# Two attention layers, experts and a binary FFN on one core: the waits that pace GpSimd's scatters, and the wait for their landing

## The chip, the core and the metric

The kernel runs on one core of a Trainium2 chip as one program. The metric is the device time of an execution in microseconds (us); "before" is the median of three runs. A profile of one execution gives the rows below.

## The reference

Four parts follow one another, each added to x (4 batches of 1024 tokens, 256 wide, f32), each on a layer norm of x: a cross attention with 77 keys and a mask, a mixture of experts with a shared expert, a second cross attention, and a feed-forward part with binary weights.

```python
x = x + _L0_xattn_ref(_layernorm(x), ctx, ctx, mask, ...)   # 16 heads of 16, 77 keys
x = x + _L0_ffn_ref(_layernorm(x), Wg, W1, W2, W3, Ws1, Ws2, Ws3)
x = x + _L1_xattn_ref(_layernorm(x), ctx, ctx, ...)
x = x + _L1_ffn_ref(_layernorm(x), k0, k1, k2, s0, s1, s2)
# in _L0_ffn_ref:
scores = softmax(xf @ Wg); weights, indices = top_k(scores, 4)      # 32 experts
for e in range(E):          # the tokens that chose e, at most C = 4 * T * 4 / 32
    out = swiglu(xf[tok], W1[e], W2[e], W3[e]) * w[:, None]
    y = y.at[tok].add(out)
z = swiglu(xf, Ws1, Ws2, Ws3)                                       # the shared expert
return y + z
```

## The kernel before

The 4096 tokens are 32 tiles of 128 rows, and four tiles make a macro tile (eight of them, m = 0 to 7). x stays in SBUF. The program is a row of blocks, and at each block's end all engines meet in a barrier: `front` (norm and queries of the first attention), `attend` (first attention), `route` (shared expert and routing), `experts`, `combine`, `attend` again (second attention) and `ffn`. Behind `attend` and `experts` the function `retire` also clears semaphores and meets in a second barrier; between `route` and `experts` it isn't called.

**Attention.** `attend` is written as 35 steps (`body`), software-pipelined over the tiles. In step t TensorE (PE) makes the scores of tile t+1, turns the probabilities of tile t in three pieces (L1008), and does `values` of tile t-1 (L1019): 30 matmuls of 51 f16 columns, each with its own 128x128 weights, 20 from PHT and 10 from PLT, into psO. Its last matmul raises `pv_done`. VectorE (DVE) opens step t with `norm` of tile t-2 (L867, L871), which waits for `pv_done` of step t-1 and raises `normed`; then come two `maximum` (L855, each raises `max_ready`), and three `low` (L862, each raises `lo_out`), with the residual between them. PE's `shift` (L997) waits for `max_ready`, so the next probabilities start from norm.

**Routing beside it.** In the first attention `Gate` does the router of macro tile m while later tiles are attended: norm by GpSimd (`power`, L1147 to L1152), turn and logits on PE (L1198, L1208), `pick` and `index` on DVE, `ranks` on PE (L1216, 14 matmuls of 32 columns), `place` and `slots` on DVE (L1270 to L1284). This ends in 16 slot numbers for each of 128 partitions. Then GpSimd (POOL) copies the macro tile's normed rows to the experts' regions of `x_rows` in HBM by 16 indirect DMAs (`scatter`, L1160): each takes 128 rows of 1072 bytes, one to a partition. Macro tiles 0 to 3 are scattered in the attention from step 4m + 15 on, four scatters to a step. `in_step` there says what each waits for: the first `normed` (norm of this step done), the others the three `lo_out` of the step. Of macro tile 4, `CUT` scatters are issued in the attention's last steps; what is left of it and macro tiles 5 to 7 are scattered in `route`. There another `in_step` paces them by PE's progress, in groups of seven to each shared-expert macro tile. The scatters of all eight macro tiles are 128.

**Route.** PE computes the shared expert of macro tile b (L1551 up, L1568 down), with the logits and ranks of macro tiles 6 and 7 in its first two turns. Its 30-odd groups are f32 matmuls of 256 or 512 columns. SyncE (SP) loads weights and the second attention's keys and values, stores zero rows behind each expert's last row ("tails", L1396) and loads W2 (L2041). At its end SP waits for the tails and POOL for the landing of every scatter.

**Experts.** SP fetches 128 rows of `x_rows` for each of 160 expert tiles (`fetch`, L1642), eight ahead. PE turns the first (L1750) and goes on from there; every expert tile's result is scattered to `y_rows` by POOL (L1657).

**The second attention** is the same `attend` without gate and scatters.

Two pieces of text that the diff doesn't show:

```python
def norm(t, u):                       # DVE, at the head of step t + 2
    dve.wait_ge(pv_done, t + 1)
    ...
def values(t, u):                     # PE, in step t + 1
    pe.wait_ge(normed, t); pe.wait_ge(lo_out, NG * t + NG)
```

Of the kernel before, what the change touches and what calls it, by code (L numbers as in the profile page):

```python
# [24 lines left out]
KC = D // P  # L25
TOKENS = BATCH * SEQ
TILES = TOKENS // P
# [26 lines left out]
GATED_EARLY, SCATTERED_EARLY, TURNED_EARLY = 6, 4, 7  # L54
CUT = 6
TURN_AT, LOGITS_AT, PICK_AT, RANKS_AT, SCATTER_AT = 8, 9, 11, 13, 15
STEPS = 7
KEYS_AT = 1
# [60 lines left out]
def build(nc, a, out):  # L119
# [605 lines left out]
    def attend(w, masked, clear_outputs, load_ahead, tail=None, gate=None):  # L725
# [73 lines left out]
        with nc.Block() as block:  # L799
# [20 lines left out]
            def _(pool):  # L820
# [12 lines left out]
                if gate:  # L833
# [3 lines left out]
                    def in_step(t, j):  # L837
                        if j == 0:
                            pool.wait_ge(normed, min(t - 1, TILES))
                        else:  # L840
                            pool.wait_ge(lo_out, min(NG * t + j, NG * TILES))
                    for m in range(SCATTERED_EARLY):
# [241 lines left out]
    class Gate:  # L1084
# [3 lines left out]
        def __init__(self, st):  # L1088
            def keep(n):
# [27 lines left out]
                keep(n) for n in ("chosen", "c_done", "ranks_read", "slots_ready", "own", "edges", "based"))  # L1117
            self.wg_in, self.w1_in = (keep(n) for n in ("wg_in", "w1_in"))
            self.scattered = [keep(f"scattered_{i}") for i in range(ROWBUFS)]
            self.own = None  # L1120
# [6 lines left out]
        def load(self, sp):  # L1127
            sp.dma_start(self.wg, a["wg"].rearrange("(c p) n -> p c n", p=P)).then_inc(self.wg_in, 16)
            sp.dma_start(self.w1, a["ws1"].rearrange("(c p) n -> p c n", p=P)).then_inc(self.w1_in, 16)

        def recycled(self, eng, m):
# [206 lines left out]
    def route(gate, counts, plan_all, own_f, next_w, load_down):  # L1338
# [25 lines left out]
            sem(s) for s in ("h_done", "silu", "hs", "z_done", "z_added", "w2_in", "plan_ready", "plan_spread", "plan_read", "w3_in"))  # L1364
        tails_s, tails_st = sem("tails_ready"), sem("tails_stored")
        own_s, plan_own = sem("own"), sem("plan_own")
# [7 lines left out]
        with nc.Block() as block:  # L1374

            @block.sync
            def _(sp):
# [19 lines left out]
                for m in range(PLAN_AT, MACROS):  # L1397
                    down(m)
                sp.wait_ge(tails_st, 16 * EXPERTS)

            @block.gpsimd
            def _(pool):
                kv.blanks(pool)

                def in_step(n):
                    b, j = divmod(n, STEPS)
                    if j in (0, 1, 4, 5):
                        pool.wait_ge(h_done, min(4 * b + (1, 2, 0, 0, 3, 4)[j], 4 * MACROS))
                    elif j in (2, 3) and b:
                        pool.wait_ge(z_done, 2 * b + j - 3)  # L1410
                gate.power(pool, MACROS - 1)
                for m in range(SCATTERED_EARLY, MACROS):
                    first = CUT if m == SCATTERED_EARLY else 0
                    gate.scatter(pool, m, first, MT * TOPK, lambda i: in_step((m - SCATTERED_EARLY) * MT * TOPK + i - CUT))
                for b in range(ROWBUFS):
                    pool.wait_ge(gate.scattered[b], SCATTERS * len(range(b, MACROS, ROWBUFS)))

# [186 lines left out]

    def experts(W13, W2, w_loaded, plan_all, own_f, binary):
        st = ExitStack()
# [22 lines left out]
        with nc.Block() as block:  # L1629

            @block.sync
            def _(sp):
                regs = [sp.alloc_register(f"first_row_{n}") for n in range(AHEAD)]

                def fetch(j, u, g):
# [6 lines left out]
                    sp.dma_start(XG[:, u, :], x_rows[ds(row, P), :]).then_inc(gathered[u], 16)  # L1642

                for j in range(ETILES):
                    fetch(j, j % AHEAD, j // AHEAD)
                    if j == AHEAD:
                        binary.load_first(sp)
                    if j == SECOND_LOAD:
                        binary.load_second(sp)
# [372 lines left out]
    with whole:  # L2022
# [24 lines left out]
        gating.close()  # L2047
        experts(W13, W2, (w_loaded, 16 * (2 * KC + 2 * MACROS)), plan_all, own_f, BinaryWeights())
        moe.close()
# [44 lines left out]
```

## Time and profile before

| what | value |
|---|---|
| median of 3 runs | 1307.51 us (1304.01 to 1314.53) |
| the profiled execution | 1310.99 us, span 1309.2 us |
| PE / DVE / ACT / POOL busy | 1179.9 / 742.6 / 516.9 / 414.3 us |
| scatters L1160 | 128, 967 to 972 ns each at the least and the median |
| first attention, route, experts (first work to last, by the rows) | 47 to 310, 311 to 417, 425 to 720 us |
| second attention | 800 to 965 us |

The busy time of an engine is a sum over stages, and it tells little of a stage in which the engines hand work to one another. How long a step of the attention lasts is read as the distance between two starts of L867. In the rows a bracket behind a row is the time for which the engine was idle before it, and what ended that; "remote" is a semaphore whose sender the profile doesn't name. An x2 behind a row counts instructions that follow each other closely, and the duration is then that of all of them.

### The profile page before, as it was taken

The page shows a single profiled execution, that of the slowest core. Times are in us where ns is not written, and L with a number is a line of the kernel's source. Part 1 is how long each engine was busy: PE and PEld are TensorE (multiplying, and loading weights), DVE is VectorE, ACT ScalarE, POOL GpSimd, SP SyncE. Part 2 cuts the span into 40 slices and gives each one's busy share as a digit, 9 for nine tenths or more (in the row PEclk, how much of TensorE's full clock was granted, in tenths as well). Part 3 has the DMA queues.
Part 4 walks back from the last instruction along what each step waited for, and adds up shares of the span by engine and source line. Part 5 has one row for each costly group of instructions (what it writes and reads, how often), then busy time and mean ns, then how long its engine had stood idle before and what let it go on. Part 6 is the DMA issues. An engine that isn't in the chain of part 4 may idle for free. (4 is left out here: it accounts for less than half of the span.)

```text
span 1309.2 us, 26064 instructions
## 1 busy us (share of the span) xinstructions
PE 1179.9 (90%) x8528; PEld 809.7 (62%) x8528; DVE 742.6 (57%) x1969; ACT 516.9 (39%) x1110; POOL 414.3 (32%) x513
## 2 busy tenths in 40 slices
PE   7799988887996899999998078999989999999998
PEld 4378766565553787777777045888855555554554
DVE  4277877764633466656566594888863343424331
ACT  6555644443211344433433155666532122213221
POOL 5260255554465355555456264300000000000000
PEclk9889999986998899999999588999999999999999
DMA  9199211112296555454442750000000000000000
GB/s 183 18 296 394 111 64 69 64 64 82 73 220 215 157 159 154 134 179 131 133 139 70 309 212 14 2 3 2 2 1 1 17 17 17 1 16 16 17 17 17
DMA packets 100993, 123.93 MB, mean 95 GB/s; under 512 B 34224, under 2 KB 76291, under 8 KB 100871
## 3 DMA queue, kind: packets, MB, share of 16 engines
q1 hardware_dynamic: 87047, 87.98, 23.0%
q0 software_dynamic: 13824, 34.38, 7.4%
q8 instruction: 71, 1.16, 0.4%
q14 instruction: 51, 0.42, 0.1%
HBM read 61.78 MB, written 64.72 MB: 97 GB/s over the span
## 5 line engine op out<-in xcount | busy, mean ns | idle before, releaser
L1971 PE MATMUL psA<-H,B 128*128 128x512 f16 x1024 | 223.5, 379 | 0.0
L1898 DVE SCALAR_TENSOR_TENSOR H<-psA,H 128x512 f16<-128x512 f32 x128 | 88.3, 690 | 208.3 <-ACT H L1939 208.3
L1657 POOL DMA_INDIRECT y_rows<-YB,pair x160 | 155.5, 972 | 147.5 <-DVE YB L1712 78.4
L1939 ACT ACTIVATE H<-psA 128x512 f16<-128x512 f32 x128 | 76.4, 597 | 252.7 <-PE psA L1971 252.7
L1971 PEld LDWEIGHTS psA<-H,B 128*128 128x128 f16 x1024 | 100.1, 98 | 119.4
L1767 PE MATMUL psH<-W,XT 128*128 x640 | 168.7, 387 | 1.6 <-issue 1.5
L940 ACT ACTIVATE PHT<-psT 128x512 f16<-128x512 f32 (+1 forms) x192 | 94.4, 524 | 129.9 <-PE psT L1008 129.9
L862 DVE TENSOR_TENSOR PLT<-psT,PHT 128x512 f16<-128x512 f32 (+1 forms) x192 | 113.9, 595 | 30.2 <-ACT PHT L940 27.3
L208 POOL TENSOR_SCALAR var<-mv 128x4 f32<-128x4 f32 x24 | 11.2, 467 | 371.2 <-DVE mv L202 370.2
L1160 POOL DMA_INDIRECT x_rows<-B,slot_s x96 | 96.2, 1002 | 84.9 <-PE psH L1551 23.1
L1767 PEld LDWEIGHTS psH<-W,XT 128*128 128x128 f32 x640 | 111.2, 194 | 12.1 <-issue 3.2
L1008 PE MATMUL psT<-ident,PR 128*128 128x128 f32 x640 | 102.9, 289 | 11.4 <-issue 5.2
L855 DVE TENSOR_REDUCE mx<-psS 128x8 fp32r<-128x616 f32 x128 | 95.9, 790 | 28.4 <-PE psS L988 28.1
L1669 ACT ACTIVATE XT<-psX 128x256 f32<-128x256 f32 x160 | 61.3, 383 | 122.7 <-PE psX L1750 90.5
L1781 PE MATMUL psY<-QT,HT 128*128 x320 | 99.8, 394 | 0.0
L1723 DVE COPY HT<-psT 128x128 f32<-128x128 f32 x159 | 46.3, 291 | 92.5 <-PE psT L1775 55.8
L932 ACT ACTIVATE PR<-psS 128x616 f32<-128x616 f32 x128 | 83.2, 690 | 38.9 <-PE psS L997 38.6
L1008 PEld LDWEIGHTS psT<-ident,PR 128*128 128x128 f32 x640 | 71.2, 145 | 34.6 <-issue 26.3
L1712 DVE TENSOR_SCALAR YB<-psY,to_gate 128x256 f32<-128x256 f32 x160 | 77.0, 482 | 11.5 <-PE psY L1781 10.5
L1750 PE MATMUL psX<-ident,XG 128*128 128x128 f32 x320 | 62.5, 278 | 15.9 <-DMA XG<-x_rows 13.2
L223 PE MATMUL psX<-ident,XN 128*128 128x128 f32 x184 | 28.4, 305 | 50.5 <-ACT XN L457 50.5
L997 PE MATMUL psS<-mx,minus_ident 128*128 128x312 f32 x256 | 62.9, 355 | 10.1 <-DVE mx L855 9.9
(248 smaller groups left out, 2054.2 us busy)
## 6 DMA issues: line engine op xcount, KB each, us to landing
XG<-x_rows SPq DMA_DIRECT2D x160, 134.0 KB
y_rows<-zero_row SPq DMA_DIRECT2D x4, 4096.0 KB, 27.2
G<-y_rows SPq DMA_DIRECT2D x7, 2048.0 KB, 10.2
x_rows<-zero_row SPq DMA_DIRECT2D x33, 134.0 KB, 7.4
X<-in_x SPq DMA_DIRECT2D x8, 512.0 KB
QT<-in_w SPq DMA_DIRECT2D x16, 256.0 KB
out_x<-OUT SPq DMA_DIRECT2D x8, 512.0 KB
y_rows<-YB,pair POOLq DMA_INDIRECT x160
```

The lines of the kernel that those rows point to most:

```text
L855: dve.tensor_reduce(m, half(h), X_AXIS, ALU.max).then_inc(max_ready, 1)
L862: dve.tensor_tensor(PLT[u][:, lo:hi], piece(t, g), PHT[u][:, lo:hi], ALU.subtract).then_inc(lo_out, 1)
L932: act.activation(PR[u][:, h * HH:(h + 1) * HH, 0:KEYS].rearrange("p (r j) k -> p r j k", r=2), half(h), ACT.Exp, scale=SCALE).then_inc(exp ...
L940: act.activation(PHT[u][:, lo:hi], piece(t, g), ACT.Copy).then_inc(hi_out, 1)
L1008: last = pe.transpose(piece(t, g)[:, c - lo], flat[:, c * P:(c + 1) * P], ident[:])
L1160: pool.indirect_dma_start(x_rows[:, :], bass.IndirectOffsetOnAxis(ap=self.slot_s[m % ROWBUFS][:, i:i + 1], axis=0), self.rows[m % ROWBUFS] ...
L1657: pool.indirect_dma_start(y_rows[:, :], bass.IndirectOffsetOnAxis(ap=pair[u // HALF][:, u % HALF:u % HALF + 1], axis=0), YB[u][:], None, b ...
L1712: dve.tensor_scalar(YB[u][:], psY[u % 2][:], to_gate[u // HALF][:, u % HALF, 1:2], None, ALU.mult).then_inc(y_out, 1)
L1767: last = pe.matmul(psH[v][:], XT[v][:, c], w13[c][:, ds(e * (2 * HID), 2 * HID)], start=c == 0, stop=c == KC - 1)
L1781: pe.matmul(psY[v][:], HT[v][:], w2[:, ds(e * D, D)], start=True, stop=True).then_inc(y_done, 1)
L1898: dve.scalar_tensor_tensor(out=H[layer][1][:, o], in0=psA[k % 4][:], scalar=0.0, in1=H[layer][0][:, o], op0=ALU.max, op1=ALU.subtract).the ...
L1971: last = pe.matmul(psA[k % 4][:], W[:, c, o * P:(o + 1) * P], src[part][:, c], start=n == 0, stop=n == 2 * n_in - 1)
```

## The change

In the first attention, the four scatters of a step wait for four other things: the first as before for `normed`; the second for the step's second `maximum`; the third for the step's second `low`; the fourth for `pv_done` of the step's `values`. Ten scatters of macro tile 4 are issued in the attention and not six, so six and not ten are left for `route`. In `route` no scatter waits for PE's progress any longer; each batch of 16 still waits for its rows, its weights and its slots. The waits for the landing of all scatters and all tails move from the end of `route` (POOL and SP) to SP's queue in `experts`, ahead of the first fetch.

```diff
--- before.py
+++ after.py
@@ -52,9 +52,8 @@
 ROWBUFS = 4
 SCATTERS = 16 * MT * TOPK
 GATED_EARLY, SCATTERED_EARLY, TURNED_EARLY = 6, 4, 7
-CUT = 6
+CUT = 10
 TURN_AT, LOGITS_AT, PICK_AT, RANKS_AT, SCATTER_AT = 8, 9, 11, 13, 15
-STEPS = 7
 KEYS_AT = 1
@@ -837,8 +836,12 @@
                     def in_step(t, j):
                         if j == 0:
                             pool.wait_ge(normed, min(t - 1, TILES))
+                        elif j == 1:
+                            pool.wait_ge(max_ready, min(2 * t + 4, 2 * TILES))
+                        elif j == 2:
+                            pool.wait_ge(lo_out, min(NG * t + 2, NG * TILES))
                         else:
-                            pool.wait_ge(lo_out, min(NG * t + j, NG * TILES))
+                            pool.wait_ge(pv_done, min(t, TILES))
                     for m in range(SCATTERED_EARLY):
                         gate.scatter(pool, m, 0, MT * TOPK, lambda i: in_step(m * MT + SCATTER_AT + i // MT, i % MT))
                         gate.power(pool, m + MT - 1)
@@ -1116,6 +1119,7 @@
+            self.tails_st = keep("tails_stored")
@@ -1127,6 +1131,11 @@
+        def all_rows(self, sp):
+            sp.wait_ge(self.tails_st, 16 * EXPERTS)
+            for b in range(ROWBUFS):
+                sp.wait_ge(self.scattered[b], SCATTERS * len(range(b, MACROS, ROWBUFS)))
@@ -1396,24 +1405,15 @@
                 for m in range(PLAN_AT, MACROS):
                     down(m)
-                sp.wait_ge(tails_st, 16 * EXPERTS)
 
             @block.gpsimd
             def _(pool):
                 kv.blanks(pool)
 
-                def in_step(n):
-                    b, j = divmod(n, STEPS)
-                    if j in (0, 1, 4, 5):
-                        pool.wait_ge(h_done, min(4 * b + (1, 2, 0, 0, 3, 4)[j], 4 * MACROS))
-                    elif j in (2, 3) and b:
-                        pool.wait_ge(z_done, 2 * b + j - 3)
                 gate.power(pool, MACROS - 1)
                 for m in range(SCATTERED_EARLY, MACROS):
                     first = CUT if m == SCATTERED_EARLY else 0
-                    gate.scatter(pool, m, first, MT * TOPK, lambda i: in_step((m - SCATTERED_EARLY) * MT * TOPK + i - CUT))
-                for b in range(ROWBUFS):
-                    pool.wait_ge(gate.scattered[b], SCATTERS * len(range(b, MACROS, ROWBUFS)))
+                    gate.scatter(pool, m, first, MT * TOPK, lambda i: None)
@@ -1641,6 +1641,7 @@
                         sp.wait_ge(met, 2 * g + u // HALF - 1)
                     sp.dma_start(XG[:, u, :], x_rows[ds(row, P), :]).then_inc(gathered[u], 16)
 
+                gate.all_rows(sp)
                 for j in range(ETILES):
                     fetch(j, j % AHEAD, j // AHEAD)
                     if j == AHEAD:
```

(`experts` takes `gate` as a further argument, and `tails_st` in `route` is now `gate.tails_st`.)

Three places on the engines' instruction lists show it. First POOL's list in the first attention, at the first macro tile's scatters (`x_rows<-B_23`). Before:

```order
L1160 DMA x_rows<-B_23,slot_s 69760x268 [waits gate_slots_ready,normed_172,gate_top_out,gate_xn_ready]
L1160 DMA x_rows<-B_23,slot_s 69760x268 [waits lo_out_169] x3
L1160 DMA x_rows<-B_23,slot_s 69760x268 [waits normed_172]
L1160 DMA x_rows<-B_23,slot_s 69760x268 [waits lo_out_169] x3
L1160 DMA x_rows<-B_23,slot_s 69760x268 [waits normed_172]
```

Now:

```order
L1169 DMA x_rows<-B_23,slot_s 69760x268 [waits gate_slots_ready,normed_172,gate_top_out,gate_xn_ready]
L1169 DMA x_rows<-B_23,slot_s 69760x268 [waits max_ready_164]
L1169 DMA x_rows<-B_23,slot_s 69760x268 [waits lo_out_169]
L1169 DMA x_rows<-B_23,slot_s 69760x268 [waits pv_done_170]
L1169 DMA x_rows<-B_23,slot_s 69760x268 [waits normed_172]
```

Of the three scatters that waited for `lo_out`, one is left, one went ahead of it and one behind the step's `values`. Second, POOL's list from the attention's end into `route`, now (before, four scatters fewer stood ahead of the first of these branches):

```order
L1169 DMA x_rows<-B_23,slot_s 69760x268 [waits pv_done_170]
L1169 DMA x_rows<-B_23,slot_s 69760x268 [waits normed_172]
L1169 DMA x_rows<-B_23,slot_s 69760x268 [waits max_ready_164]
L798 UNCONDITIONAL_BRANCH
L132 ISA [waits barrier_Pool_Activation_PE_DVE_SP_gather]
...
L1169 DMA x_rows<-B_23,slot_s 69760x268 [waits gate_slots_ready,gate_top_out,gate_xn_ready]
L1169 DMA x_rows<-B_23,slot_s 69760x268 x5
L1169 DMA x_rows<-B_23,slot_s 69760x268 [waits gate_slots_ready,gate_top_out,gate_xn_ready]
L1169 DMA x_rows<-B_23,slot_s 69760x268 x15
...
L1383 UNCONDITIONAL_BRANCH
```

The last scatters of the attention now stand behind `pv_done` and `normed` of its last tile, and the branch that ends `route` has no waits; before it read:

```order
L1374 UNCONDITIONAL_BRANCH [waits gate_scattered_2,gate_scattered_3,gate_scattered_1,gate_scattered_0]
```

Third, SP's list where `experts` begins, now:

```order
L1383 UNCONDITIONAL_BRANCH
L1631 UNCONDITIONAL_BRANCH [waits barrier_Pool_Activation_PE_DVE_SP_release]
L1637 TENSOR_LOAD plan_all [waits gate_scattered_2,gate_scattered_1,gate_scattered_3,gate_scattered_0,gate_tails_stored]
L1638 ISA
L1642 DMA XG<-x_rows 128x268
```

The load of the row numbers, and so every fetch, carries the waits that stood ahead of the barrier.

## Rows read from the trace of the kernel before

**Rows 1.** Timeline of VectorE, first attention: start us, duration us, instruction [idle before]; heads of steps.

```profile
129.70 0.22 DVE L867 RECIPROCAL rden<-psO 128x16 f32<-128x16 f32 x1
...
156.71 0.25 DVE L867 RECIPROCAL rden<-psO 128x16 f32<-128x16 f32 x1
...
239.57 0.26 DVE L867 RECIPROCAL rden<-psO 128x16 f32<-128x16 f32 x1 [2.27 <-remote]
...
247.53 0.26 DVE L867 RECIPROCAL rden<-psO 128x16 f32<-128x16 f32 x1 [3.45 <-remote]
...
291.15 0.25 DVE L867 RECIPROCAL rden<-psO 128x16 f32<-128x16 f32 x1
```

**Rows 2.** Waits, 150 to 300 us: us in total, times, longest.

```profile
DVE rden L867 <- remote: 32.9, 15, 3.5
```

**Rows 3.** Timeline of the second attention: end of `values` and the next step's head.

```profile
867.32 0.18 PE L1019 MATMUL psO<-V,PLT 128*128 128x51 f16 x1
...
867.68 0.25 DVE L867 RECIPROCAL rden<-psO 128x16 f32<-128x16 f32 x1
```

**Rows 4.** Timeline of PE and POOL in two steps of the first attention with scatters.

```profile
237.09 0.19 PE L1019 MATMUL psO<-V,PLT 128*128 128x51 f16 x1
...
237.86 0.97 POOL L1160 DMA_INDIRECT x_rows<-B,slot_s  x1 [0.30 <-issue]
...
241.09 0.97 POOL L1160 DMA_INDIRECT x_rows<-B,slot_s  x1 [2.25 <-DVE CX L871]
...
243.02 0.21 PE L1019 MATMUL psO<-V,PHT 128*128 128x51 f16 x2
...
243.09 0.97 POOL L1160 DMA_INDIRECT x_rows<-B,slot_s  x1 [1.04 <-DVE PLT L862]
...
245.65 0.97 POOL L1160 DMA_INDIRECT x_rows<-B,slot_s  x1 [0.30 <-issue]
```

**Rows 5.** Timeline of DVE: the end of `slots` in a step without scatters.

```profile
156.63 0.17 DVE L1284 CAST slot_s<-B 128x16 int32<-128x16 f32 x1
```

**Rows 6.** Timeline where the first attention ends and `route` begins: POOL, DVE, SP.

```profile
300.81 0.97 POOL L1160 DMA_INDIRECT x_rows<-B,slot_s  x1 [0.31 <-issue]
...
302.79 0.26 DVE L867 RECIPROCAL rden<-psO 128x16 f32<-128x16 f32 x1 [3.82 <-remote]
...
309.65 0.17 DVE L1284 CAST slot_s<-B 128x16 int32<-128x16 f32 x1
...
311.45 0.38 SPq L1378 DMA_DIRECT2D B<-in_ws  x1
```

**Rows 7.** Timeline where `experts` ends and `combine` begins: POOL, SP.

```profile
719.07 0.97 POOL L1657 DMA_INDIRECT y_rows<-YB,pair  x1 [0.30 <-issue]
...
725.78 0.90 SPq L673 DMA_DIRECT2D G<-y_rows  x2
```

**Rows 8.** Timeline of `route`: DVE and PE, early and in the middle.

```profile
326.59 0.29 DVE L1270 TENSOR_TENSOR B<-psR,base 128x128 f32<-128x128 f32 x1 [2.23 <-remote]
...
327.49 5.38 PE L1551 MATMUL psH<-QT,B 128*128 128x512 f32 x8
...
332.70 3.62 PE L1568 MATMUL psZ<-w,HS 128*128 128x256 f32 x16
...
370.49 3.62 PE L1568 MATMUL psZ<-w,HS 128*128 128x256 f32 x16
```

**Rows 9.** Timeline where `route` ends and `experts` begins: SP, DVE, POOL, PE.

```profile
400.22 9.81 SPq L2041 DMA_DIRECT2D QT<-in_w  x12
...
413.77 0.69 DVE L1471 TENSOR_TENSOR X<-X,psZ 128x512 f32<-128x512 f32 x1 [0.78 <-PE psZ L1568]
...
416.10 0.97 POOL L1160 DMA_INDIRECT x_rows<-rows,slot_s  x1 [0.30 <-issue]
...
424.58 0.94 SPq L1642 DMA_DIRECT2D XG<-x_rows  x2
...
426.72 0.69 PE L1750 MATMUL psX<-ident,XG 128*128 128x128 f32 x2 [12.99 <-DMA XG<-x_rows]
```

More of the change, by code:

```diff
@@ L1364, in route @@
             sem(s) for s in ("h_done", "silu", "hs", "z_done", "z_added", "w2_in", "plan_ready", "plan_spread", "plan_read", "w3_in"))
-        tails_s, tails_st = sem("tails_ready"), sem("tails_stored")
+        tails_s, tails_st = sem("tails_ready"), gate.tails_st
         own_s, plan_own = sem("own"), sem("plan_own")
@@ L1603, in route, with experts @@
         st.close()
-    def experts(W13, W2, w_loaded, plan_all, own_f, binary):
+    def experts(W13, W2, w_loaded, plan_all, own_f, binary, gate):
         st = ExitStack()
@@ L2047, in build @@
         gating.close()
-        experts(W13, W2, (w_loaded, 16 * (2 * KC + 2 * MACROS)), plan_all, own_f, BinaryWeights())
+        experts(W13, W2, (w_loaded, 16 * (2 * KC + 2 * MACROS)), plan_all, own_f, BinaryWeights(), gate)
         moe.close()
```

## The prediction

> **What bounds the kernel now.** I read the page's slices first, then the waits, then the timeline of the places that the edits touch. About 1% (13 us) is what a measurement of this kernel can tell from no change. The sums are made against the profiled execution, 1310.99 us, which lies 3.5 above the median 1307.51.
>
> The first attention hands work round between the engines, and a step is read from one L867 to the next. Four steps without scatters take 156.71 - 129.70 = 27.0 us. From there to 291.15 lie 16 steps, in which four macro tiles are scattered: 134.4 us, 33.6 for four [rows 1]. The router's work is the same in both. In the waits DVE stands at L867 for a "remote" semaphore 15 times, 32.9 us in all [rows 2]. L867 waits for `pv_done`, the end of PE's `values`. In the second attention, with no scatters, `values` ends at 867.32 + 0.18 = 867.50 and L867 starts 0.18 later [rows 3]. In the first one `values` is recorded as ended at 237.28, and L867 starts at 239.57 [rows 4, 1]: 2.29 us. That stretch is the time in which POOL runs the last of its back-to-back scatters, start 237.86, and L867 follows 1.71 after that start. So my reading is that a group of small matmuls with many weight loads doesn't finish, or its count isn't seen, while scatters follow one another without a gap; the recorded end of PE is modelled and hides this. DVE waits, and everything of the next step hangs on its norm.
>
> Where do the three scatters behind `lo_out` fall? In the step of 239.57 the first goes at 241.09 behind the norm, the second at 243.09 behind the first `low`, the fourth at 245.65; a scatter lasts 0.97 and the next one starts 0.30 behind it, so 1.28 each [rows 4]. `values` begins at 243.02. Three back-to-back scatters lie on it, all ahead of `pv_done`, and the next L867 comes at 247.53, 1.88 behind the last one's start [rows 1, 4]. The step is 7.96 long.
>
> In `route` the f32 groups don't show this: L1568 x16 takes 3.62 us at 332.70 among spaced scatters and 3.62 at 370.49 among back-to-back ones [rows 8]. A small group does: DVE waits 2.23 "remote" for ranks (L1270, 326.59), and the L1551 group behind it is recorded at 5.38 us for eight matmuls [rows 8].
>
> The end of `route`: DVE's last work ends at 413.77 + 0.69 = 414.46, POOL's last scatter at 417.07. The first fetch is issued at 424.58 and PE starts at 426.72 after 12.99 us idle [rows 9].
>
> **Attention, spacing.** One of three scatters that lay ahead of `pv_done` now lies behind it. Take `pv_done` at 0: the fourth scatter starts at about 0.8 (the start of 241.09 is 1.52 behind L867 at 239.57 and L871 lies between, so a wake-up takes 0.8), the first of the next step at 2.1 by POOL's spacing, then 3.4 and 4.6, since their waits (second maximum, second `low`) are met by then. `values` lies at 3.5 to 4.4. The release comes 1.75 (mean of 1.71 and 1.88) behind the last: 6.4. Before, it was 7.96, and the difference is one spacing, 1.28, and some. Per four steps I get 6.4 for two steps with nothing else, and 15 for the two that also carry the router's work, of which one is bound by DVE anyway: in the cycle without scatters, `slots` ends at 156.63 + 0.17 and L867 is there at 156.71 [rows 5, 1]. Together some 28 to 28.5 against 33.6: 5.1 to 5.6, times four is 20 to 22. I take **-20**. The most it can give is 134.4 - 108.0 = 26.4 (four cycles at 27.0); the least, if the wait comes of any scatter near `values` and not of their row, is 0, or worse by nothing that these rows show, since each step has the same four scatters.
>
> **Attention, the end.** Four more scatters run behind `normed` and `pv_done` of the last tile. The last one of before starts at 300.81; DVE ends at 309.65 + 0.17 = 309.82, and `route`'s first work is at 311.45, 1.6 later: POOL wasn't the bound [rows 6]. Now the row of POOL begins with the last `pv_done`, seen at 302.79 [rows 6]: four scatters from 0.5 on end at about 307.1. A block whose end hangs on a scatter is seen twice: experts' last scatter ends at 720.04 and `combine` starts at 725.78, 5.7 later [rows 7]; route's 417.07 and 424.58, 7.5 later, there with waits for the landing [rows 9]. 307.1 + 5.7 = 312.8 to 307.1 + 7.5 = 314.6, against 311.45: +1.4 to +3.2. I take **+2**; 0 if POOL's drain runs beside DVE's tail, 4 at worst.
>
> **Route, unpaced scatters.** 54 scatters at 1.28 are 69 us: from 314 to 383, not to 417.07. The f32 groups cost nothing by [rows 8]. The ranks of macro tile 7, which sat between spaced scatters, now fall into a row of them: one wait like that of macro tile 6, 2.23 us, with 1.8 of PE behind it (5.38 for x8 of 512 columns against 3.62 for x16 of 256, the same columns). I take **+2**, bounds 0 and 5. The transfers to HBM are fewer beside W2 at the end than before, which costs nothing I can see.
>
> **Route, the end.** POOL and SP no longer hold the barrier. What is last is DVE's 414.46. At the attention's end it took 1.6 from DVE's last work to the next block's first [rows 6], there with a clearing that isn't done here: 414.46 + 0.5 to 1.6 is 415.0 to 416.1, against 424.58: -8.5 to -9.6. The moved waits are long met: the last scatter ends at about 383 and the tails are ahead of the W2 loads in SP's queue [rows 9]. SP has the load of W2 behind it at 400.22 + 9.81 = 410.03. Queued behind the moved waits are the row numbers and every fetch; if these waits weren't met, PE would wait for them as now. I take **-9**.
>
> Sum: -20 + 2 + 2 - 9 = -25: **1286 profiled, 1283 as a median**.
>
> **A rule against it.** The rows show DVE held 2.3 us behind `values` only where scatters run [rows 1, 3, 4]. The Trainium skill (SBUF — State Buffer, "SBUF: two separate sides") says that inside the engines' side only the port pair of DVE and GpSimd contends, and that TensorE never waits on anyone. By it PE couldn't be held by a scatter, and moving scatters past `pv_done` would give nothing in the attention. The sum doesn't use it; it is the first rival's mechanism.
>
> **Rivals.**
> 1. Spacing gives nothing. L867's "remote" wait comes with the four scatters of a step, not with three in a row: what holds it is their number, and the new fourth scatter, behind `pv_done`, only joins the next step's three, so POOL runs the same row of four. For it: POOL is busy 5.1 us of a step either way, and after the change no gap is left in the row. Against: 6.4 of POOL's row ends earlier. Time: +2 + 2 - 9 = -5: **1302.5**.
> 2. `values` isn't held at all any more, for its row of scatters is broken: four cycles at 27.0, -26.4 + 2 + 0 - 9 = -33: **1274**. Against: POOL has the work of 5.1 us in 6.7, so a scatter lies on `values` always.
> 3. Slower. In `route`, unpaced scatters hold PE's groups as they do in the attention, which stretched four steps by 33.6/27.0 = 1.24: 69 us would hold 69 - 69/1.24 = 13.4 more. With no gain in the attention: -9 + 2 + 13.4 = +6.4; with the ranks at +5 as well, +11: **1314 to 1319**. It decides from 5 us of PE held on. For it: the 2.23 and the 5.38 [rows 8]. Against: 3.62 in both kinds of stretch.
> 4. The change doesn't spread the scatters: the second and third waits are met when POOL comes to them, so the four go out in one row from `pv_done` on. My step already counts with that; where the row then also reaches past the next `pv_done`, POOL paces the steps and it ends as rival 1.
>
> **Chances.** Forecast 0.50 (1276 to 1292: the attention -26 to -12, its end 0 to +4, the ranks 0 to +5). Rival 2 0.17, rival 1 and 4 0.25 (1295 to 1306), rival 3 0.08. The range: 1271 (all of rival 2 but its last few us) to 1302, which leaves out rival 3, a third of rival 1 and little else: under 2 in 10. Faster by over 1% (under 1294.4): the forecast, rival 2 and a little of 1: 0.70. Within 1%: 0.23. Slower by over 1% (over 1320.6): only the upper end of rival 3 and what no row shows: 0.07.
>
> **What would show it.** L867 to L867: 27.5 to 29 us for four steps between 156 and 285, and the "remote" total of L867 well under 20 us; 33 says rival 1, 27 rival 2. The last L1160 of `route` at about 375 to 385, L1568 x16 still at 3.62; a longer one is rival 3. The gap between DVE's last work of `route` and the first L1642 at 0.5 to 1.6 us. The gap between the attention and `route`, from DVE's last work to L1378, at 1.6 to 5. I am wrong if small groups are held by something other than rows of scatters, if the landing of W2 or of the scatters comes late, or if the fetches' first rows meet a queue that the earlier scatters filled.

## The result, and the profile after

The change is slower: 1329.36 us (median of 4 runs, 1326.96 to 1341.93) against 1309.59, ratio 1.0172 with a 95% interval of 1.0094 to 1.0249. The forecast was 1283. The experiments then showed that these runs belong to one of two conditions, and that what scatters cost TensorE differs between them by some 50 us for the very same kernel; I call them **held** (the runs of before at 1304 to 1315 us) and **free** (at 1255 to 1263 us). In the free one the change is not told apart from before: 1255.72 against 1257.74, ratio 0.9988, 0.9946 to 1.0029. First the profile of the change in the held condition (the profiled execution 1330.2 us, span 1328.5; lines moved by 3 to 9).

VectorE's timeline, heads of steps, as in [rows 1]. A cycle below is four steps, in which the 16 scatters of one macro tile are issued.

```profile
156.64 0.25 DVE L870 RECIPROCAL rden<-psO 128x16 f32<-128x16 f32 x1
...
162.98 0.26 DVE L870 RECIPROCAL rden<-psO 128x16 f32<-128x16 f32 x1
...
169.69 0.26 DVE L870 RECIPROCAL rden<-psO 128x16 f32<-128x16 f32 x1 [0.85 <-PE psO L1022]
...
176.72 0.26 DVE L870 RECIPROCAL rden<-psO 128x16 f32<-128x16 f32 x1 [0.75 <-PE psO L1225]
...
189.33 0.25 DVE L870 RECIPROCAL rden<-psO 128x16 f32<-128x16 f32 x1
...
286.27 0.25 DVE L870 RECIPROCAL rden<-psO 128x16 f32<-128x16 f32 x1
```

Three steps of this cycle last 6.3, 6.7 and 7.0 us (forecast: 6.4 for two of them), where they lasted about 7.9. The fourth, with the logits and ranks, lasts 12.6 against 9.6; in the four cycles it takes 12.6, 10.9, 12.6 and 10.9 us. Four cycles take 286.27 - 156.64 = 129.6 us, and took 134.4 [rows 1].

The attention's end and the beginning of `route`, as in [rows 6]: VectorE, SyncE.

```profile
306.23 0.17 DVE L1293 CAST slot_s<-B 128x16 int32<-128x16 f32 x1
```

```profile
311.04 0.38 SPq L1387 DMA_DIRECT2D B<-in_ws  x1
```

4.6 us from the one's end to the other, against 1.6.

Waits, 310 to 440 us (us in total, times, longest):

```profile
DVE B L1248 <- remote: 30.9, 1, 30.9
...
DVE B L1279 <- remote: 7.9, 1, 7.9
```

L1248 reads the logits of macro tile 7. The timeline of PE around them, and of POOL:

```profile
325.44 1.94 PE L1217 MATMUL psX<-B,QT 128*128 128x32 f32 x16 [0.93 <-ACT QT L1518]
327.22 5.38 PE L1551 MATMUL psH<-QT,B 128*128 128x512 f32 x8
...
342.55 0.58 PE L1568 MATMUL psZ<-w,HS 128*128 128x256 f32 x1 [1.51 <-issue]
344.65 0.59 PE L1568 MATMUL psZ<-w,HS 128*128 128x256 f32 x1 [1.51 <-issue]
347.45 0.59 PE L1568 MATMUL psZ<-w,HS 128*128 128x256 f32 x1 [2.21 <-issue]
349.56 1.01 PE L1551 MATMUL psH<-QT,B 128*128 128x512 f32 x1 [1.53 <-issue]
352.35 1.01 PE L1551 MATMUL psH<-QT,B 128*128 128x512 f32 x1 [1.78 <-issue]
```

```profile
360.57 0.97 POOL L1169 DMA_INDIRECT x_rows<-B,slot_s  x1 [0.30 <-issue]
361.85 0.97 POOL L1169 DMA_INDIRECT x_rows<-B,slot_s  x1 [0.30 <-issue]
376.77 0.97 POOL L1169 DMA_INDIRECT x_rows<-rows,slot_s  x1 [13.95 <-DVE slot_s L1293]
```

```profile
365.67 0.29 DVE L1248 TENSOR_REDUCE B<-psX 128x4 f32<-128x128 f32 x1 [30.86 <-remote]
```

The logits group is recorded as ended at 327.38 and VectorE reads it at 365.67, 2.9 us after the row of scatters pauses (361.85 + 0.97). The trace also keeps the times at which semaphores were raised: the count that L1248 waits for stands at 365.64. So it isn't VectorE that is late; the count itself comes 38.3 us behind the recorded end. Meanwhile TensorE gets through one matmul in 2.1 to 2.8 us, waiting for "issue". The windows of 334 to 362 and 362 to 370 us (PE, PEld, DVE, ACT, POOL busy; granted clock; DMA; GB/s) show what that does:

```profile
334.00:362.00 28.00, 8.24 (x14) 3.00 (x12) 0.77 (x2) 0.00 (x0) 21.30 (x23) 0.58 0.29 105
362.00:370.00 8.00, 1.41 (x2) 0.84 (x3) 3.72 (x21) 3.65 (x10) 0.82 (x1) 0.50 0.09 34
```

PE works 8 of 28 us, and the granted clock falls from 2.4 to 1.2 GHz in that stretch. POOL stopped only because the last slots hung on those logits.

The end of `route`, as in [rows 9]: VectorE, SyncE, PE.

```profile
448.77 0.69 DVE L1471 TENSOR_TENSOR X<-X,psZ 128x512 f32<-128x512 f32 x1 [0.78 <-PE psZ L1568]
450.60 2.35 SPq L1642 DMA_DIRECT2D XG<-x_rows  x4
...
452.77 0.48 PE L1751 MATMUL psX<-ident,XG 128*128 128x128 f32 x1 [4.04 <-DMA XG<-x_rows]
```

From VectorE's end to the first fetch it is now 1.1 us; it was 10.1. This part came as forecast.

| change in us, before to after | held | free |
|---|---|---|
| up to the head of step 156 | -0.1 | -1.4 |
| from there to VectorE's end in the attention | -3.3 | 0.0 |
| to `route`'s first load | +3.0 | +4.7 |
| to VectorE's end in `route` | +35.4 | -0.8 |
| to the first fetch | -9.0 | -9.0 |
| experts, to the first load of `combine` | -8.0 | +1.3 |
| the rest | +1.3 | +0.2 |
| span | +19.3 | -5.1 |

(The free column is from one profiled execution each, 1259.65 and 1254.55 us.) Why the experts are 8 us shorter in the held column isn't settled: in the five other held profiles, that of before among them, they last 298 to 307 us, in free ones 280, so they are held too, and by a varying amount; what sets that amount was not tested.

### The profile page after: what moved, and what is told of

The parts are those of the page before. It is cut to its first block and busy times, and to the rows that moved or that the text cites. A ratio compares the mean times of both kernels' runs of the same rounds, so it can differ in the third digit from the quotient of the medians.

```text
span 1328.5 us, 26058 instructions
## 1 busy us (share of the span) xinstructions
PE 1176.0 (89%) x8528; PEld 815.3 (61%) x8528; DVE 742.9 (56%) x1969; ACT 517.1 (39%) x1110; POOL 411.1 (31%) x513
## 5 line engine op out<-in xcount | busy, mean ns | idle before, releaser
L858 DVE TENSOR_REDUCE mx<-psS 128x8 fp32r<-128x616 f32 x128 | 96.0, 792 | 29.7 <-PE psS L991 29.6
L935 ACT ACTIVATE PR<-psS 128x616 f32<-128x616 f32 x128 | 82.5, 689 | 36.7 <-PE psS L1000 36.0
L1551 PE MATMUL psH<-QT,B 128*128 128x512 f32 x128 | 64.9, 653 | 18.6 <-ACT SG L1514 12.4
L1042 PE MATMUL psM<-wo,CT 128*128 128x256 f32 x256 | 69.9, 397 | 0.6 <-ACT CT L949 0.5
```

The costliest lines, as they stand in the source:

```text
L858: dve.tensor_reduce(m, half(h), X_AXIS, ALU.max).then_inc(max_ready, 1)
L935: act.activation(PR[u][:, h * HH:(h + 1) * HH, 0:KEYS].rearrange("p (r j) k -> p r j k", r=2), half(h), ACT.Exp, scale=SCALE).then_inc(exp ...
```

## The experiments

Each is an edit of the kernel before unless it says otherwise. Ratios are against before in the same comparison.

**1. The parts alone.** `land`: only the landing waits are moved. `route`: only

```diff
-  gate.scatter(pool, m, first, MT * TOPK, lambda i: in_step((m - SCATTERED_EARLY) * MT * TOPK + i - CUT))
+  gate.scatter(pool, m, first, MT * TOPK, lambda i: None)
```

`attn`: only the four waits in the attention and `CUT = 10`. `attn_land`: `attn` and `land`.

> Only the waits for the landing of scatters and tails are moved to SyncE's queue behind the barrier; scatters are issued and paced as before. Theory: this part works as predicted and is worth the gap at route's end. POOL's last scatter still ends at about 417, so the barrier is left by POOL 1 to 5 us behind that: first fetch at 418 to 422 instead of 424.6, 3 to 6 us less in all. Rival: the drain of POOL and not the wait for the landing makes the gap; then the first fetch stays at 424 and the time is the same within 1 us.

> Only the pacing in route is taken away (48 + 10 scatters back to back); attention and landing waits as before. Theory: an unbroken row of scatters starves TensorE, and this one edit is the loss: the logits of macro tile 7 are seen over 25 us late, route's matmuls come one by one at about 2 us, and the kernel is 20 to 30 us slower than before. Rival: it takes the ten scatters of the attention with it (other positions, four more at the end); then this kernel is within 8 us of before.

> Only the attention's part: the new waits of the second to fourth scatter and ten instead of six scatters of macro tile 4; route paced and landing waits as before. Theory: the three steps without router work get 1.1 us shorter each, the fourth 1 to 3 us longer, so the attention ends about 3 us earlier and the kernel is 2 to 5 us faster than before. Rival: four scatters fewer in route also let route end 6 us earlier, since POOL is the last there: 8 to 10 us faster.

> Attention's part and moved landing waits together, route paced: the change without the unpaced scatters. Theory: the parts add up: route ends with DVE at 411 to 414, the first fetch comes 1 to 2 us behind it, 10 to 14 us faster than before, and 30 us faster than the change. Rival: the paced scatters still end last in route; then only 5 to 8 us faster than before.

Before took 1258.49 us here (22 runs). `land` 1258.2, ratio 0.9998 (0.9987 to 1.0009): nothing, as its rival said. POOL's last scatter still ends at 385.6 and the first fetch comes at 391.5. `route` 1251.45, 0.9929 (0.9907 to 0.9950): some 7 to 9 us faster, where 20 to 30 us slower was expected. `attn` 1258.22, 0.9982 (0.9965 to 0.9998) and `attn_land` 1256.21, 0.9980 (0.9962 to 0.9998): some 2 us, and under 5 by the intervals. All four have cycles of 26.8 us and no remote wait at L867. So neither the hold nor its cure could be seen here, and my account of the first profile stood untested.

**2. The change and the kernel before again.**

> The change itself, once more. In the four partial kernels no wait of VectorE behind TensorE's small groups was seen while scatters ran, and the route part alone was 7 us faster than before; in the change's first profile such waits were 5 to 31 us long. Theory: whether rows of scatters hold TensorE's completions depends on the chip or its condition at the time, not on the combination of the parts. Then either this run has no such wait and is 6 to 10 us faster than before, or it has them and is 15 to 25 us slower, and the kernel before beside it shows the same condition (four-step cycle 27 or 33.5 us). Rival: only the combination of parts does it; then the change is slower here while the kernel before has cycles of 27 us.

> The kernel before, once more, for its profile beside that of the change on the same chip. Theory: it has remote waits at L867 (cycle 33.5 us, about 1308 us) exactly where the change is slower, and none (cycle 27 us, about 1258 us) where it is faster. Rival: its cycle says nothing about the change's result.

The two numbers are given above: free, cycles of 26.8 in both. VectorE's timeline in the kernel before, of a profile without any hold:

```profile
156.70 0.25 DVE L867 RECIPROCAL rden<-psO 128x16 f32<-128x16 f32 x1
...
163.04 0.26 DVE L867 RECIPROCAL rden<-psO 128x16 f32<-128x16 f32 x1
...
168.73 0.26 DVE L867 RECIPROCAL rden<-psO 128x16 f32<-128x16 f32 x1
...
174.40 0.24 DVE L867 RECIPROCAL rden<-psO 128x16 f32<-128x16 f32 x1
...
183.55 0.25 DVE L867 RECIPROCAL rden<-psO 128x16 f32<-128x16 f32 x1
...
263.90 0.25 DVE L867 RECIPROCAL rden<-psO 128x16 f32<-128x16 f32 x1
```

263.90 - 156.70 = 107.2 us for the 16 steps that took 134.4 in [rows 1], with the same scatters, four to a step. The combination isn't needed for the hold, nor enough for it. The span differs by 1309.2 - 1257.9 = 51.3 us: 29.7 from the head at 156.7 to VectorE's end in the attention, 0.2 from there to the first fetch, 21.7 in the experts, and -0.3 elsewhere. The two stages in which POOL scatters beside many short groups of TensorE hold it all; the second attention and `ffn` are alike. The scatters' packets take as long in both: in the queue's rows of the 16 steps (packets, MB, share of 16 engines), before in its first profile over 133.3 us, and again over 105.3 us,

```profile
q0 software_dynamic: 2991, 8.58, 17.9%
```

```profile
q0 software_dynamic: 2928, 8.37, 22.1%
```

133.3 x 16 x 0.179 / 2991 = 0.128 us a packet, and 105.3 x 16 x 0.221 / 2928 = 0.127. So it isn't slower transfers that hold TensorE.

The kept traces differ in one more way. Both of before record all 26064 instructions, but not as many raised semaphores: from the head at 156.7 to the attention's end 1067 held and 1678 free, in `route` 1250 and 2238, in the experts 3007 and 6851, and elsewhere the same within one (1314 and 1314 ahead of it, 2186 and 2187 behind). Most of the missing ones are the DMAs' own. On the page it shows as a fetch without a time to its landing, first before, then before again:

```profile
XG<-x_rows SPq DMA_DIRECT2D x160, 134.0 KB
```

```profile
XG<-x_rows SPq DMA_DIRECT2D x160, 134.0 KB, 2.5
```

All six held profiles of this document lack this time, and all fourteen free ones have it (2.3 to 2.6 us). Records are missing exactly in the stages with indirect DMAs, so either raised semaphores as such are disturbed there, or their recording is. Whether an execution without a recording knows the hold at all is a rival that no run here tests.

**3. A later start of the row.** `late`: `route`'s edit, and POOL waits ahead of it for the read of the last logits (`pool.wait_ge(gate.l_shift, MACROS)`). `late_b` is the same once more.

> Route's scatters back to back as in the change, but the row starts only when VectorE has read the last logits (13 us later); attention and landing waits as before. Two conditions have been seen: one in which scatters hold TensorE's completions (before about 1308 us), one in which they don't (before about 1258 us). In the first: if only small groups of matmuls open the backlog, the logits wait of 31 us is gone, one wait of the last ranks remains, and route is within 5 us of before, the kernel 2 to 8 us faster; if f32 groups are held as well, route is 15 us or more longer. In the second: the row ends at about 373 instead of 359, still ahead of VectorE's last work, so as fast as the unpaced kernel, 5 to 8 us faster than before.

> Route's scatters back to back, but the row starts only when VectorE has read the last logits, once more; the rest as before. Where scatters hold TensorE (before at about 1313 us): if only groups of many small matmuls open the backlog, the logits wait of 31 us is gone and what is left is the ranks of the last macro tile, a wait of 2 to 25 us by VectorE at L1270, and L1568 x16 stays at 3.6 us outside it: route 105 to 125 us long. If f32 groups are held as well by an unbroken row, they come one matmul at a time over the whole row of 74 us and route is 135 us or longer, as without the late start (145). Where they don't hold it: 103.7 as before seen.

Free both times. `late` 1252.06, 0.9941 (0.9921 to 0.9962), `late_b` 1255.25 beside 1259.77 (one run). The row ended at 375 to 376 (expected: 373), ahead of VectorE's 385. What it does in the held condition stays untried.

**4. The change without its attention part** (`route_land`), and **pauses between scatters.** Ahead of each scatter of route (`gap`), or of the second to fourth of an attention step in place of its wait (`attn_gap`), two memsets of a spare 128x32 tile:

```diff
+        def pause(self, pool):
+            for _ in range(2):
+                pool.wait_ge(self.gap_s, self.gaps)
+                pool.memset(self.gap[:], 0.0).then_inc(self.gap_s, 1)
+                self.gaps += 1
```

> Route's scatters back to back and the landing waits moved, attention and the six scatters of macro tile 4 as before: the change without its attention part. Where scatters don't hold TensorE: the moved waits give nothing more, since POOL and the landing are 25 us ahead of VectorE already; 6 to 8 us faster than before, as the route part alone, and 3 to 5 us faster than the change, which pays for four scatters behind the attention's last tile. Rival: the two edits add up, and it is 9 us or more faster. Where scatters do hold TensorE: 20 us or more slower than before.

> Route's scatters unpaced, but two small memsets of POOL that wait for one another ahead of each, so that no two scatters stand back to back; the rest as before. Where scatters hold TensorE (before at about 1308 us): if it is the unbroken row that does it, the logits wait is gone and route ends with POOL at about 410 to 415; if POOL's scatters hold it at any spacing, it is over 15 us slower. Where they don't (before about 1258 us): 58 scatters at 1.9 us end at about 395, behind VectorE's last work, and the kernel is within 3 us of before.

> In the attention the second to fourth scatter of a step wait for nothing but two small memsets of POOL ahead of each; the rest as before. Where scatters hold TensorE: if an unbroken row does it, the remote waits at L867 go and the four-step cycle falls from 33.5 us to 28 to 30, the kernel 14 to 20 us faster; otherwise it stays at 33. Where they don't: the cycle is 26.8 us as without any scatters, and the time that of before within 2 us.

Free. `route_land` 1252.09, 0.9945 (0.9925 to 0.9965): the parts of the end don't add up, since the early end of the scatters alone removes the gap. `gap` 1273.1 beside 1258.72, and `attn_gap` 1277.38: both expectations of "no more than 2 or 3 us" were wrong. The gap between scatters grew from 0.30 to 0.95 us, 1.92 a scatter. In `route` 58 of them end at 398.7 and the fetch at 406.5 waits for them; in the attention 7.0 us a step is more than the 6.7 that a step lasts, and the last two cycles came to 31.4 and 32.4. Where nothing is held, pauses only make POOL the bound.

**5. One burst, and rows of eight.** `burst`: in the attention, of a macro tile's 16 scatters only the first waits. `row8`: `route` unpaced, with six such memsets ahead of every eighth scatter.

> In the attention only the first scatter of each macro tile waits for its step; the other 15 follow back to back, 20 us in a row, and POOL rests for the remaining steps of the cycle. The rest as before. Where scatters hold TensorE (before at about 1308 us): if an unbroken row is what does it, three steps of a cycle stand together behind one wait of L867 of 10 us or more, and the cycle is over 33 us; if it is their number at a step's values, the steps are as before. Where they don't (before about 1258 us): cycles of 27 us and the time of before within 2 us.

> Route's scatters unpaced, but after every eight a pause of about 2 us (six small memsets that wait for one another). Where scatters hold TensorE: the backlog is worked off in each pause, the logits are late by at most 10 us instead of 31, and route is within 8 us of before. Where they don't: the row ends at about 372, ahead of VectorE, and the kernel is 5 to 8 us faster than before.

Held this time: before 1315.41. `burst` 1354.87 (one run). VectorE's timeline in it:

```profile
155.56 0.25 DVE L869 RECIPROCAL rden<-psO 128x16 f32<-128x16 f32 x1
...
201.21 0.25 DVE L869 RECIPROCAL rden<-psO 128x16 f32<-128x16 f32 x1
```

Cycles of 45.7, 45.6, 45.2 and 44.8 us, with as many scatters in each as in the 33.5 of before and the 26.8 of the free runs. So it is not their number but that they follow without a gap, and POOL's rest behind the burst doesn't give it back. Some of the length is TensorE's clock (PE busy, granted clock of the first cycle):

```profile
155.56:201.21 45.65, 29.66 (x320) 22.79 (x319) 23.90 (x68) 15.94 (x37) 17.79 (x21) 0.78 0.14 49
```

PE idles 16.0 us of the cycle, and the fall of the clock comes with that; how the excess over 33.5 us divides between the two isn't shown. `row8` 1327.28 (one run): its waits, 310 to 450 us,

```profile
ACT SG L1521 <- remote: 39.1, 4, 15.4
```

and the timeline of PE and ACT around two of these four waits:

```profile
347.11 3.60 PE L1558 MATMUL psH<-QT,B 128*128 128x512 f32 x8
...
353.14 0.60 ACT L1521 ACTIVATE SG<-psH 128x512 f32<-128x512 f32 x1 [10.40 <-remote]
...
379.39 3.64 PE L1558 MATMUL psH<-QT,B 128*128 128x512 f32 x8
...
391.68 0.60 ACT L1521 ACTIVATE SG<-psH 128x512 f32<-128x512 f32 x1 [15.41 <-remote]
```

The ranks were read at 327.2, in the first pause behind eight scatters (325.8 to 327.5), and the logits at 329.9 without a wait, instead of at 365.7. But ScalarE waited four times for f32 groups. The group of 379.39 is recorded as ended at 383.03, after the usual 3.64 us, and its count is raised at 391.65 by the trace, 0.03 ahead of ScalarE's start. So f32 groups are held too, and such a group's own duration doesn't show it. `route` took 122.2 us from its first load to the first fetch, against 113.1 before (the gap of its end no longer in it): 9.1 over, just past the 8 expected.

**6. The route part, and the pauses in the attention, held.**

> The route part alone, once more: no pacing in route, attention and landing waits as before. Where scatters don't hold TensorE it was 7 us faster than before. Where they do (before at about 1310 us): theory: this edit alone is the loss, the logits are seen 25 to 31 us late, and route takes 136 to 142 us from its first load to the first fetch, against 113 before and 139.6 in the change. Rival: the loss needs the ten scatters in the attention; then route is within 5 us of 113.

> The attention's scatters with two small memsets ahead of the second to fourth of a step instead of their waits, once more. Where scatters don't hold TensorE, POOL's row of 7 us a step made cycles of 27 to 32 us. Where they do: if it is the unbroken row, the remote waits at L867 of 1.7 to 3.5 us in every step are gone or under 1 us, and the cycle is at most 31 us against 33.5; if scatters hold TensorE at any spacing of this size, the waits stay and the cycle is 33 us or more.

Held: before 1313.15. `route_b` 1346.87 (one run), 33.7 us slower, the same edit that gained 7 where nothing is held. `route` takes 145.1 us to the first fetch, with 1.0 from VectorE's end to it, and the wait is that of the change:

```profile
DVE B L1239 <- remote: 31.5, 1, 31.5
```

`attn_gap_b` 1297.36 (one run), 15.8 us faster than before beside it, the same edit that cost 19 in the free condition. Waits, 156 to 320 us:

```profile
DVE rden L867 <- remote: 8.9, 4, 2.8
```

against 36.7 in 16 for before in the same window (32.9 in 15 up to 300 us [rows 2]). Its cycles are 27.5, 28.9, 28.9 and 32.9 us; the last is the longest in the free run too (32.4), where POOL is the bound. A gap of 0.95 us between scatters ends most of the hold. These two ran on a chip with the same number as `gap` and `attn_gap`, which were free: the condition isn't a fixed property of the chip with that number.

**7. The open rest.** `gap_b` is `gap` again; `attn_gap1` has one memset instead of two in the attention; `gap1_late` is `attn_gap1` with `late`.

> Route's scatters with two small memsets ahead of each, without any pacing by TensorE, once more. Where scatters hold TensorE: with gaps of 0.95 us no backlog builds up, no remote wait in route is over 3 us, and route is bound by POOL's row as where they don't hold it: 122 to 127 us. Rival: the number of scatters while small groups run is what counts; then the logits are 10 us late or more and route is over 130 us.

> The attention's second to fourth scatter of a step with one small memset ahead of each (a gap of about 0.6 us, 6.1 us of POOL a step) instead of two (0.95 us, 7.0 us a step). Where scatters hold TensorE: POOL no longer bounds the steps, so if 0.6 us is gap enough the cycle falls below that with two (29.6 us mean) to 28, the kernel 20 us faster than before; if not, waits of over 1.5 us at L867 return and the cycle is over 31 us. Where they don't hold it: cycle 27, the time of before.

> Two edits in two stages: in the attention one small memset ahead of the second to fourth scatter of a step (a gap of 0.6 us) in place of their waits; in route the scatters back to back, but only from the read of the last logits on. Where scatters don't hold TensorE: cycles of 27 us and route 104 us, together 5 to 8 us faster than before, as the late row alone. Where they do: the attention's cycle is 28 us if 0.6 us is gap enough, over 31 if not; route is 105 to 125 us if only small groups open the backlog, 135 or more if an unbroken row also holds f32 groups.

All free. `gap_b` 1276.52 beside 1259.77; `attn_gap1` 1259.39 beside 1259.77, cycles of 26.8, so one memset costs nothing; `gap1_late` 1250.68, 0.9936 (0.9918 to 0.9954), 8 us faster than before, where the change's ratio is 0.9988. Their held side wasn't had.

## Why the prediction was wrong

**The reading under all of it.** That L867's remote wait comes of scatters in an unbroken row was right for the trace I had (`burst`, `attn_gap_b`). That it is a property of the kernel was not: I took one execution's condition for the program's, and nothing in the text asks how the 27.0 us of a cycle "without scatters" would look with them in another execution. It looks the same: in the free profile of before the cycle without scatters is 27.0 and those with them are 26.8. The Trainium skill (SBUF — State Buffer, "SBUF: two separate sides") says that TensorE waits on no other engine there. The free profiles agree (27.0 without and 26.8 with scatters). In the held ones TensorE's groups are late (cycles of 45 in `burst`), but whether SBUF has a part in that no run tells.

**Attention, spacing: -20; measured held -4.8 over the 16 steps (-3.3 to VectorE's end), free 0.** The failing step is "15 for the two that also carry the router's work": held, they took 7.0 + 12.6 = 19.6 in the first cycle and 17.7 to 19.4 in the others, against 17.5 to 18.1 before. The steps without router work missed by less: 6.3 to 7.2, 6.9 on average, for 6.4 worked out and 7.9 before. (6.4 + 6.4 + 15 is also 27.8 and not "28 to 28.5".)

What the 15 had at nothing is TensorE's clock. The fourth steps of the change, then one of before and one of the change when free (PE busy in the second place, the granted clock third from the end):

```profile
176.72:189.33 12.61, 12.61 (x117) 10.62 (x117) 7.94 (x22) 3.20 (x7) 5.25 (x5) 0.73 0.13 45
210.29:221.14 10.85, 10.85 (x116) 9.24 (x116) 7.94 (x22) 3.19 (x7) 5.21 (x5) 0.84 0.14 52
241.84:254.41 12.57, 12.57 (x117) 10.59 (x117) 7.93 (x22) 3.20 (x7) 5.20 (x5) 0.73 0.12 46
275.32:286.27 10.95, 10.25 (x98) 8.37 (x97) 7.92 (x22) 4.27 (x9) 5.21 (x5) 0.84 0.16 52
```

```profile
214.06:223.64 9.58, 8.21 (x97) 5.71 (x95) 7.77 (x22) 3.25 (x7) 4.48 (x7) 1.00 0.15 55
```

```profile
172.94:182.08 9.14, 8.98 (x112) 7.40 (x112) 7.73 (x23) 3.29 (x8) 5.06 (x6) 1.00 0.22 76
```

PE is busy for nearly all of these steps, and part of each runs at 1.2 GHz. Length times granted clock is 9.2, 9.1, 9.2 and 9.2 us, an estimate of the same work at 2.4 GHz, and the free step is 9.14. So the fourth step isn't longer by scatters that lie on it: some 10.3 of the 15.2 us that the 16 steps fell short of -20 are the clock, by this estimate. In before the clock fell in the first and the last fourth step alone (0.82 and 0.69), and these took 9.7 and 10.2 us beside 9.6 in the other two. Ahead of the first fall in the change PE had been busy 5.4 of 7.0 us (169.69 to 176.72). Why the clock falls in every cycle of the change wasn't tested.

**Attention, the end: +2, measured +3.0 held, +4.7 free.** From the last scatter's end to `route`'s first load it is 7.4 us in both (303.64 to 311.04, 277.94 to 285.33), at the upper end of my 5.7 to 7.5; held, VectorE ends 2.8 us behind that scatter and covers more of it than free, 0.7 us behind. The size came out, and in part by luck: by the prediction's own spacing four scatters from 0.5 behind 302.79 end at 308.1, and not at 307.1.

**Route, unpaced: +2, measured +35.4 held, -0.8 free.** This is the step that turned the sign. "The f32 groups cost nothing by [rows 8]" rested on recorded durations, and in `row8` a group of 3.64 us has its count raised 8.6 us behind its recorded end, with ScalarE waiting 15.4. The duration doesn't say when the count comes; the wait of the engine behind it does. In [rows 8] the wait of 2.23 and the 5.38 were the sign, and I priced them once. In the free profile of before both are gone:

```profile
296.57 0.29 DVE L1270 TENSOR_TENSOR B<-psR,base 128x128 f32<-128x128 f32 x1 [0.46 <-PE psR L1216]
...
299.24 3.68 PE L1551 MATMUL psH<-QT,B 128*128 128x512 f32 x8
```

From `route`'s first load to VectorE's end PE is busy 107.3 of 138.4 us in the change and 100.4 of 103.0 in before: 28.5 of the 35.4 us are idle time of PE, and the rest goes with its lower clock (0.84 granted against 0.95). Rival 3 had the place and the sign, but at 13 us from a ratio of cycles, and decided against by the same durations. `route_b`, one held execution, shows that this edit alone makes the loss.

**Route, the end: -9, measured -9.0 in both.** The right size for half a reason: `land` shows that moving the waits is worth nothing alone, `route` (free) and `route_b` (held) that the early end of the scatters is worth all of it: 1.0 us from VectorE's end to the first fetch in both, with the landing waits where they were.

Rival 1 (spacing gives nothing, 1302.5) had the free outcome's form for the attention. That its -5 is also the difference of the two free spans (-5.1) is luck: +4.7, -9.0 and +1.3 make that up, and the medians differ by 2.

## What to carry over

Ask of a wait that the profile puts down to "remote" whether it is the kernel's or the execution's: a second profile of the same kernel, taken at another time, answers it before any edit is priced, and here it would have shown 51 us between two executions. A fetch without a time to its landing was the mark on the page here. Judge whether a group is held by the wait of its consumer, not by its own recorded duration. Look at the granted clock of the steps that a sum rests on: a step in which TensorE is nearly always busy grows with every fall of it. An edit that packs GpSimd's scatters gained 7 us in one condition and lost 34 in the other, and pauses cost 19 us in one and gained 16 in the other (the held side from one execution each): a version for both has to be measured in both.

## What the runs showed of the hardware

- Two conditions in which the same program takes 1258 and 1310 us on one core, lasting for all executions of a comparison, not tied to the chip's number. In one of them, and only there, the semaphores that TensorE's groups raise come late while POOL issues indirect DMAs 0.30 us apart: 38.3 us behind the recorded end in the change, and 42.8 in `route_b` (327.67 and 370.49).
- In that condition TensorE got through one matmul per 2.1 to 2.8 us in the last 20 us of a row of 38 such scatters, and the late count was raised 2.8 us after the row's pause. Rows of eight with pauses of 1.7 us between them made `route`'s work 121.2 us, against 144.1 with the unbroken row (`route_b`) and 102.3 with the same row when free; gaps of 0.95 us between single scatters took VectorE's waits at L867 from 36.7 us to 8.9.
- The change's fourth steps, with TensorE busy for nearly all of them, took 12.6, 10.9, 12.6 and 10.9 us at a mean granted clock of 0.73, 0.84, 0.73 and 0.84, and 9.1 at full clock.
- What makes the condition isn't known. It doesn't show in the transfers' times (0.128 and 0.127 us a packet), but in the records of raised semaphores: 1067 against 1678 in the attention's 16 steps and its end, 3007 against 6851 in the experts, and the same number where no indirect DMA runs.
